# LSTM step: the recurrent product split into one of 64 columns for g and i and one of 64x64 for o, with one tanh for o

## The reference, cut to what matters

```
def step(carry, xs):
    h, c = carry
    xi_t, xf_t, xg_t, xo_t = xs
    i_t = sigmoid(xi_t + h @ V_i)
    f_t = sigmoid(xf_t + h @ V_f)
    g_t = tanh(xg_t + h @ V_c)
    o_t = sigmoid(xo_t + h @ V_o)
    c_new = h * c + i_t * g_t
    h_new = o_t * tanh(c_new)
    return ((h_new, c_new), h_new)
```

## Time and profile before

| | |
|---|---|
| median of 3 runs | 4113.29 us |
| profiled execution, its own time | 4112.39 us |
| its span, first to last instruction | 4110.3 us |
| mean granted TensorE clock | 0.713 of full speed |
| PE busy | 2859.4 us, 70% |
| DVE busy | 2522.9 us, 61% |
| ACT busy | 1935.8 us, 47% |
| POOL busy | 959.0 us, 23% |

### The profile page before, as it was taken

The page is one execution under the profiler, slowest core; times in us unless marked ns, Lnnn a source line. Parts: engine busy times, 40 slices in busy tenths (PEclk is TensorE's granted clock), DMA queues, the critical chain, the costliest instruction groups (busy, mean ns, idle before and its releaser), DMA issues. The chain is left out here.

```text
span 4110.3 us, 62810 instructions
## 1 busy us (share of the span) xinstructions
PE 2859.4 (70%) x15784; PEld 2127.8 (52%) x15784; DVE 2522.9 (61%) x10119; ACT 1935.8 (47%) x6903; POOL 959.0 (23%) x1515
## 2 busy tenths in 40 slices
PE   4777667667677767776667777676544919999666
PEld 2555555555555555555555555555432406666555
DVE  5666666666666666666666666665445973333787
ACT  1455555555555555555555555555544422323322
POOL 2332222222222222222222222221102930000110
PEclk9777666666776766666677667665556959989777
DMA  2000000000000000000000000000001000000000
GB/s 80 11 24 14 16 16 15 25 15 15 15 14 15 15 15 16 16 25 15 15 15 15 15 15 15 16 16 20 10 2 22 0 8 3 5 5 0 6 8 8
DMA packets 54595, 61.27 MB, mean 15 GB/s; under 512 B 26576, under 2 KB 45136, under 8 KB 53840
## 3 DMA queue, kind: packets, MB, share of 16 engines
q1 hardware_dynamic: 54224, 57.07, 4.6%
HBM read 42.35 MB, written 4.19 MB: 11 GB/s over the span
## 5 line engine op out<-in xcount | busy, mean ns | idle before, releaser
L1037 PE MATMUL psL<-r_h,lvab 128*96 128x16 f32 x2048 | 446.7, 297 | 777.0 <-DVE r_h L1066 730.4
L1037 PEld LDWEIGHTS psL<-r_h,lvab 128*96 128x96 f32 x2048 | 363.2, 228 | 1011.9 <-DVE r_h L1066 942.9
L1060 DVE TENSOR_TENSOR_SCAN r_c<-r_wk 64x24 f32<-64x24 f32 x1024 | 261.2, 255 | 601.7 <-ACT r_wk L1046 593.4
L1046 ACT ACTIVATE r_wk<-psL 64x16 f32<-64x16 f32 x1024 | 189.1, 185 | 909.5 <-PE psL L1037 908.1
L1066 DVE SCALAR_TENSOR_TENSOR r_h<-r_wk,r_tc 64x8 f32<-64x8 f32 x2048 | 357.5, 175 | 355.8 <-ACT r_tc L1051 338.8
L1048 ACT ACTIVATE r_wk<-psL 32x8 f32<-32x8 f32 x2048 | 357.3, 174 | 37.0
L1051 ACT ACTIVATE r_tc<-r_c 64x8 f32<-64x8 f32 x1024 | 214.8, 210 | 262.4 <-DVE r_c L1060 249.2
L584 POOL TENSOR_TENSOR a_xw<-a_S,a_dtm 128x512 f32<-128x512 f32 x128 | 156.5, 1241 | 299.1 <-DVE a_dtm L510 299.1
L1069 DVE SCALAR_TENSOR_TENSOR r_wk<-r_h,r_c 64x8 f32<-64x8 f32 x1024 | 188.9, 184 | 35.6
L926 PE MATMUL psC<-m_xT,W 128*128 128x256 f32 x512 | 199.6, 489 | 1.0 <-ACT m_h L955 1.0
L1403 DVE SCALAR_TENSOR_TENSOR Y<-img,W,Y 128x512 f32<-128x512 f32 x147 | 185.0, 1311 | 9.1 <-DVE Y L1403 8.9
(11 more groups left out here) (396 smaller groups left out, 7059.9 us busy)
## 6 DMA issues: line engine op xcount, KB each, us to landing
accb<-acc_in SPq DMA_DIRECT2D x64, 512.0 KB, 4.1
a_xy<-a_E SPq DMA_DIRECT2D x512, 16.0 KB, 1.8
W<-pack_in SPq DMA_DIRECT2D x1, 3165.0 KB, 13.2
x6d<-X SPq DMA_DIRECT2D x64, 32.0 KB
ys<-Y SPq DMA_DIRECT2D x8, 256.0 KB, 2.9
out_x<-X SPq DMA_DIRECT2D x32, 64.0 KB, 1.6
X<-x_in SPq DMA_DIRECT2D x1, 1856.0 KB, 17.8
W<-pack_in SPq DMA_DIRECT2D x1, 1331.0 KB, 5.6
```

The lines of the kernel that those rows point to most:

```text
L1037: nc.tensor.matmul(psL[0:RM, par, c:c + 2 * LB], lvab[:], h, start=False, stop=False, skip_group_check=True).then_inc(sem("r_z"), 1)
L1046: nc.scalar.activation(o, psL[0:64, par, c:c + 2 * LB].rearrange("p (g b) -> p g b", b=LB), ACT.Tanh).then_inc(sem("r_gi"), 1)
L1060: v.tensor_tensor_scan(r_c3[:, t % 2, :], r_wk[:, 0:24], r_wk[:, 30:54], 0.0, ALU.mult, ALU.add).then_inc(sem("r_c"), 1)
```

## The change

TensorE now does two matmuls a step. The first has the weights of g and i alone, 128 x 64, with the same h. The second has the 64 x 64 weights of o (`lvo`, new) and h in partitions 0 to 63, columns 0 to 7, and writes partitions 64 to 127 of the bank, columns 0 to 7 of the step. Each adds one to `r_z`, so ScalarE waits for 2n - 1 before the tanh of g and i, and for 2n before that of o, which is one instruction of 64 partitions x 8. The input matmul L1013 has 128 columns (g and all of o) and L1015 has 64 (i). The scaling of the weights follows the new layout. Buffers, semaphores and the order of everything else stay as they are.

```diff
-        lua = resident("lua", 65, RM)
-        lub = resident("lub", 65, RM)
-        lvab = resident("lvab", P, RM)
+        lua = resident("lua", 65, P)
+        lub = resident("lub", 65, 64)
+        lvab = resident("lvab", P, 64)
+        lvo = resident("lvo", 64, 64)
...
-            nc.tensor.matmul(ps[0:RM, :, 0], lua[:], xv, start=True, stop=False, skip_group_check=True)
+            nc.tensor.matmul(ps[:, :, 0], lua[:], xv, start=True, stop=False, skip_group_check=True)
             yield SLOT["r"]["xp"][1]
-            nc.tensor.matmul(ps[0:RM, :, 1], lub[:], xv, start=False, stop=False, skip_group_check=True).then_inc(sem("r_xp"), 1)
+            nc.tensor.matmul(ps[0:64, :, 1], lub[:], xv, start=False, stop=False, skip_group_check=True).then_inc(sem("r_xp"), 1)
...
-                nc.tensor.matmul(psL[0:RM, par, c:c + 2 * LB], lvab[:], h, start=False, stop=False, skip_group_check=True).then_inc(sem("r_z"), 1)
+                nc.tensor.matmul(psL[0:64, par, c:c + 2 * LB], lvab[:], h, start=False, stop=False, skip_group_check=True).then_inc(sem("r_z"), 1)
+                nc.tensor.matmul(psL[64:P, par, c:c + LB], lvo[:], h[0:64, 0:LB], start=False, stop=False, skip_group_check=True).then_inc(sem("r_z"), 1)
...
-                act.wait_ge(sem("r_z"), n)
+                act.wait_ge(sem("r_z"), 2 * n - 1)
                 o = r_wk[:, 2:2 + 84].rearrange("p (g x) -> p g x", x=28)[:, 0:2, 0:24:3]
                 nc.scalar.activation(o, psL[0:64, par, c:c + 2 * LB].rearrange("p (g b) -> p g b", b=LB), ACT.Tanh).then_inc(sem("r_gi"), 1)
-                for s in range(2):
-                    nc.scalar.activation(TO[32 * s:32 * s + 32], psL[64:RM, par, c + s * LB:c + (s + 1) * LB], ACT.Tanh)
+                act.wait_ge(sem("r_z"), 2 * n)
+                nc.scalar.activation(TO, psL[64:P, par, c:c + LB], ACT.Tanh)
...
-                v.tensor_scalar(lub[:], w("ub"), 0.5, None, ALU.mult)
-                v.tensor_scalar(lvab[0:64, 64:RM], w("vab", 64, RM)[0:64], 0.25, None, ALU.mult)
-                v.tensor_scalar(lvab[64:P], w("vab")[64:P], 0.25, None, ALU.mult)
-                v.tensor_scalar(lvab[0:64, 0:64], w("vab", 0, 64)[0:64], 0.5, None, ALU.mult)
+                v.tensor_scalar(lua[:, RM:P], w("ub", 64, RM), 0.5, None, ALU.mult)
+                v.tensor_scalar(lub[:], w("ub", 0, 64), 0.5, None, ALU.mult)
+                v.tensor_scalar(lvab[0:64], w("vab", 0, 64)[0:64], 0.5, None, ALU.mult)
+                v.tensor_scalar(lvab[64:P], w("vab", 0, 64)[64:P], 0.25, None, ALU.mult)
+                v.tensor_scalar(lvo[:, 0:32], w("vab", 64, RM)[0:64], 0.25, None, ALU.mult)
+                v.tensor_scalar(lvo[:, 32:64], w("vab", 64, RM)[64:P], 0.25, None, ALU.mult)
```

## The result

The changed kernel took 4234.68 us (median of 4, 4223.44 to 4243.84) against 4112.49 of the kernel before: ratio 1.0298, 95% interval 1.0266 to 1.0329. So it is 122 us slower. The forecast was +53: slower was right, but the size was under half of what was measured.

What follows compares the result with a forecast made beforehand. The prediction took a chain of waits in the LSTM recurrence, with three engines the limit in turn, to bound the kernel. Narrower loads -29, second product +109 and +14, one tanh -41 gave +53 us, 4165 us; range 4066 to 4235.

Steps and rivals of the forecast that it cites:

- Bound: Recurrence: TensorE, ScalarE and VectorE limit in turn; TensorE waited for h before 736 of 1024 steps, late in 288.
- The shape: TensorE, between the two products: going from 128x64 to 64x64 was taken to stop the queue, like the 0.10 us change seen.
- Rival A: The two products overlap side by side in different array columns: sum -45 us, 4067 us, faster; chance 0.2.
- The holds: TensorE's time held by both products together: 0.66 us instead of 0.34 at 1.2 GHz, 0.42 instead of 0.20 at 2.4.
- The stop in front: TensorE, ahead of the first product behind full-width work: 0.10 us, hidden where TensorE waits for h.
- Lone step: An LSTM step at the end with no other work in the queues: from 1.75 to about 1.6 us.
- Waits for h: Steps in which TensorE waits for h before the recurrent product: should fall from 736 towards 600.
- One tanh: ScalarE, one tanh instruction for o instead of two: 0.11 us in 372 steps, 41 us gained.
- The wait for o: ScalarE, o's tanh waits for the second product, leaving a gain of 0.07 or 0.19 us, 0.11 in the mix.
- the second product's price: TensorE: 0.38 us more in 288 late steps, 109 us, plus 14 us for a tenth of the 736 waiting steps.
- the clock as a risk: TensorE: if the granted clock rises clearly above 0.68, the sum is too high; no size was set.
- Rival C: A late TensorE makes ScalarE and VectorE late with other work: +188 us, some 4250 us in the middle; chance 0.14.

Runs made afterwards that it cites:

- e4: The kernel before with a 64x32 product nobody reads behind each recurrent product, and one input product padded to 128 columns: 4183.30 us, ratio 1.0173.
- f2: The kernel before with a second product of the same 128x96 shape, zero weights, read by nobody: 4185.54 us, ratio 1.0176.
- e1: The changed kernel with o's weights padded by zeros to 128 rows, so both products have the shape 128x64: 4047.79 us, ratio 0.9855.
- f3: e1 with o's tanh again in two pieces of 32 partitions: 4100.56 us, ratio 0.9972.
- e2: The changed kernel with o's tanh again in two pieces of 32 partitions: 4328.14 us, ratio 1.0530.
- f1: e1 with a third product, 64x64 with zero weights, into the other bank, read by nobody: 4228.03 us, ratio 1.0290.
- f4: The changed kernel run again, unchanged, in a second job: 4223.38 us, ratio 1.0266.
- h4: The changed kernel with an unread bf16 product of zeros ahead of TensorE's wait for h in steps 1 to 3 and 9 to 11 of a row: 4176.35 us.
- g4: e1 with a third product, 128x96 with zero weights, into the other bank: 4212.23 us, ratio 1.0243.
- g1: The changed kernel with the first product padded by zero columns to 96, and one input product padded to 128 columns: 4176.49 us, ratio 1.0149.

## Why the prediction was half right

- Bound (three engines in turn, TensorE late in 288 steps): right. e4 and f2 priced TensorE's time at 73/0.27 = 270 and 75/0.27 = 280 us per us of hold; the prediction's 288 steps and half of 74 more are 325, near enough.
- The shape: right, and it was the point that decided. The rule of the Trainium skill, page TensorEngine Tiling (Array Packing), section Key Properties, that changing the tiling mode drains TensorE agrees with the trace for 128x64 to 64x64 too (0.32 us from the first product's start to o's). The rule of the Trainium skill, page TensorE: Matmul & The Clock Gate, section Part 3: Packing small matmuls, that products in distinct column groups run concurrently agrees with the traces only where the shape is the same (e1, starts 0.007 us apart). Rival A's time, 4067, was e1's within 20 us.
- The holds: 0.66 and 0.42 forecast, 0.64 and 0.43 measured, so 0.27 more in the mix where 0.28 was forecast. o's product starts 0.20 and 0.14 us after the second pass of the first, as forecast. The stop in front: 0.10 forecast, 0.14 and 0.09 measured behind full-width work.
- Lone step 1.6 forecast, 1.58 measured. Waits for h "towards 600": 623.
- One tanh: 41 forecast, 53 measured with o in time (f3 against e1), 93 to 105 with o late (e2 against the changed kernel). Mis-sized downwards, so it can't explain the loss. The wait for o, which had cut this term from 0.187 to 0.11 us, cost nothing (f1 against f4).
- **The step that failed** is the second product's price: 0.38 us more in 288 late steps, 109 us, and 14 for the others, with the clock's mix of 36% at 2.4 GHz taken from the earlier trace rows and held fixed. The microseconds per step were right; what they cost was not. Forecast and rival A, which differ almost only in this price, lie 98 us apart; the changed kernel and e1, which differ in the shape of the second product alone, lie 176 to 187 apart. The prediction named the clock as a risk, but in the other direction ("if the granted clock rises"). It fell to 0.63. The hold it adds depends little on that (0.30 at 1.2 GHz, 0.24 at 2.4); TensorE's other work does, and it stands in the queue ahead of the product. The 6th step of a row went from never long to 2.4 us longer in 14 of 26 rows, the 13th from 1.4 to 1.6 us longer in 8 rows to 1.6 to 3.2 in 14. That is 60 us of the 79 between the forecast and the profiled execution, and 52 of 60 in f4's. Fillers ahead of just these steps raised the clock there and took 47 to 58 us back (h4), and the sums of these two steps moved with them (218.6 to 172.0 us). That the clock is what lengthens these steps rests on this and on the granted clock of the changed kernel's steps: 0.50 in every long 6th step, 0.50 to 0.88 in the long 13th steps, 1.00 in all short ones.
- Rival C gave the delay's spread 0.14 and 4250 us: its size was near, its mechanism (ScalarE late with other work, nothing from the tanh) was not what happened.

What stays open: why the clock falls. In the runs above it was 0.61 to 0.64 in the window 1000 to 2000 us where the first product has 64 columns and the hold is long (changed kernel, f1, g4), and 0.67 where the first has 96 columns (e4, f2, g1) or the hold is short (e1). But the first group also keeps TensorE longest once the stop in front is counted, 0.99 to 1.02 us behind full-width work at 1.2 GHz against at most 0.95. The shape and the total time were not separated; the runs show the pairing, not the cause.

Open too is a part of what the third product cost on e1: 172 (f1) and 188 us (g4) between the profiled executions. The 6th and 13th steps explain 57 and 67, the price found on the kernel before (75) as much again; some 40 remain. Where e1 is less held up by ScalarE, TensorE's time may weigh more; that was not isolated.

## What to carry to other kernels

Before splitting a small product over the array's columns, give all parts the same number of rows of weights (what was varied here; the columns were equal), padding with zeros if need be: with the padded o product the kernel was 62 us faster than before (e1), with the exact 64x64 one it was 176 to 187 us slower than that. In a chain of waits, price an engine's added time by the steps in which that engine was late, not by its busy share, and expect that to be too low where the engine is only just in time: on the kernel before it held (270 to 280 us per us, 288 late steps), on e1, with 316 late steps, nearly the same hold cost more than twice as much. One reason is the clock, so don't hold TensorE's fixed in such a sum: look at the granted clock step by step, and ask which steps have queued work ahead of the link and are only just in time.

## What the runs showed of the hardware that was not expected

- The granted clock in one and the same step of the program was 1.00 or 0.50 from row to row, and the step 3.12 or 5.48 us, in one execution.
- The clock fell (0.68 to 0.63 in the window 1000 to 2000 us) while TensorE's busy share there rose (71% to 81%). Busy time in the profile counts the standstill at a change of shape: in the lone step the first product's record lasts 0.39 us and covers the 0.32 until o's product starts.
- Six filler products of zeros per row, 192 in all, made the changed kernel 47 to 58 us faster (h4). Three per row on e1 changed nothing that is clear of the intervals (4047.79 to 4041.20).
- fp32 passes of two products alternate in the array when their shapes agree, starts 0.007 us apart in the median over e1's steps.
- A change of shape in TensorE's queue cost 0.14 us at 1.2 GHz and 0.09 at 2.4 behind full-width work, and none where the recurrent product had 96 columns instead of 64.
